# Attention and channel mixing on one core: parts of the beginning reordered, a later pace in the last unit, two projection blocks moved from unit 1 to unit 0

## What is computed

```
x = x + layernorm(attention(layernorm(x)))
    q, k, v = x @ w_q.T, x @ w_k.T, x @ w_v.T          # 16 heads of 16
    out = softmax(q k^T / 4) v;  out @ w_o.T
x = x + layernorm(ffn(layernorm(x)))
    xr, xk = mixes of x with the token before it (mu_r, mu_k)
    sigmoid(xr @ W_r.T) * (square(relu(xk @ W_k.T)) @ W_v.T)
```

## Time and profile before

| | before |
|---|---|
| median of 3 runs | 1273.29 us (1273.29 to 1273.8) |
| the profiled execution's own time | 1274.69 us |
| its span, first to last instruction | 1272.9 us |
| PE matmuls busy | 1252.4 us (98%) |
| ACT busy | 1067.7 us (84%) |
| DVE busy | 779.1 us (61%) |
| POOL busy | 276.4 us (22%) |
| mean granted TensorE clock | 0.998 |

### The profile page before, as it was taken

How to read it: one execution, slowest core, us unless ns; L and a number is a source line. 1 busy time by engine, 2 the same in 40 slices (tenths; PEclk the granted TensorE clock), 3 DMA queues, 4 the chain that set the end, 5 groups by cost and what they waited for, 6 DMA issues and landing times.

```text
span 1272.9 us, 25486 instructions
## 1 busy us (share of the span) xinstructions
PE 1252.4 (98%) x10604; PEld 603.3 (47%) x10604; DVE 779.1 (61%) x1725; ACT 1067.7 (84%) x1159; POOL 276.4 (22%) x356
## 2 busy tenths in 40 slices
PE   8999999999999999999999999999999999999997
PEld 5544454454544444454544544444444445534344
DVE  6543747758465773847567584666747466463737
ACT  4788888888888888888888888888888888898872
POOL 3000212222211321222121221223222122222211
PEclk9999999999999999999999999999999999999999
DMA  4455553317712194124733166321871129400001
GB/s 153 115 144 166 98 129 78 101 51 126 124 52 84 52 180 87 52 66 106 144 68 113 42 116 125 73 84 51 143 124 51 35 75 174 85 1 20 15 1 34
DMA packets 61797, 112.70 MB, mean 89 GB/s; under 512 B 6512, under 2 KB 31344, under 8 KB 61616
## 3 DMA queue, kind: packets, MB, share of 16 engines
q1 hardware_dynamic: 61360, 109.60, 38.8%
q10 hardware_dynamic: 288, 1.05, 0.3%
HBM read 68.42 MB, written 41.94 MB: 87 GB/s over the span
## 4 chain that ended last, share of the span: by engine, by line
PE 93%; DVE 3%; ACT 2%; DMA 1%; POOL 0%; issue 0%; ACTq 0%; DVEq 0%
PE O L602 38%; PE S L583 26%; PE M L353 14%; PE M L340 11%; PE M L250 3%; ACT PT L590 1%; DVE sth L701 1%; DMA A<-w_dram 1%; PE M L483 1%; DVE A L710 0%; PE S L1016 0%; POOL rsh L706 0%; DVE QS L474 0%; ACT QS L471 0%; DVE A L914 0%
## 5 line engine op out<-in xcount | busy, mean ns | idle before, releaser
L590 ACT ACTIVATE PT<-S 128x1024 f32<-128x1024 f32 x1024 | 1003.5, 1026 | 156.8 <-PE S L583 156.2
L602 PE MATMUL O<-PT,V 128*17 128x512 f32 x4096 | 538.9, 598 | 0.0
L583 PE MATMUL S<-QS,KS 50*128 50x512 f32 x2048 | 465.4, 450 | 3.2 <-ACT PT L590 3.2
L583 PEld LDWEIGHTS S<-QS,KS 50*128 50x128 f32 x2048 | 211.0, 183 | 452.7 <-ACT PT L590 375.2
L602 PEld LDWEIGHTS O<-PT,V 128*17 128x17 f32 x4096 | 67.8, 95 | 139.5 <-issue 137.7
L705 POOL TENSOR_SCALAR veh<-mvh 128x2 f32<-128x2 f32 x96 | 22.3, 232 | 491.3 <-DVE mvh L703 490.1
L914 DVE SCALAR_TENSOR_TENSOR A<-Z,M 128x512 f32<-128x512 f32 x30 | 20.4, 682 | 159.6 <-PE M L353 159.6
L340 PE MATMUL M<-xnT,WH 64*128 64x512 f32 (+1 forms) x504 | 110.7, 393 | 1.1 <-DVE WL L985 1.1
L353 PE MATMUL M<-WH,xnT 64*128 64x256 f32 (+1 forms) x496 | 83.0, 278 | 0.0
L353 PE MATMUL M<-WH,cT 64*128 64x256 f32 (+1 forms) x496 | 82.1, 278 | 0.5 <-DVE rec L661 0.4
L353 PE MATMUL M<-WH,C 64*128 64x256 f32 (+1 forms) x496 | 81.8, 278 | 0.0
(11 more groups left out here) (130 smaller groups left out, 1610.0 us busy)
## 6 DMA issues: line engine op xcount, KB each, us to landing
scr<-p SPq DMA_DIRECT2D x124, 256.0 KB
QS<-scr SPq DMA_DIRECT2D x56, 256.0 KB, 6.7
KS<-scr SPq DMA_DIRECT2D x56, 256.0 KB, 11.0
QS<-scr SPq DMA_DIRECT2D x70, 128.0 KB, 6.0
KS<-scr SPq DMA_DIRECT2D x68, 128.0 KB, 8.5
xA<-x_dram SPq DMA_DIRECT2D x16, 512.0 KB, 7.0
xB<-x_dram SPq DMA_DIRECT2D x16, 512.0 KB, 7.2
out_dram<-xB SPq DMA_DIRECT2D x15, 512.0 KB, 3.4
```

The lines of the kernel that those rows point to most:

```text
L583: fn = lambda e, p=p, a=a, rows=rows: e.matmul(PS[p][:, a, :], KS[qd][rows, p, kt * 128:kt * 128 + 128], QS[qd][rows, p, hf * 512:hf * 512 ...
L590: e_fn = lambda e, p=p: e.activation(PT[i % 2][:, 2 * p:2 * p + 2, :], PS[p][:, :, :], ACT.Exp, scale=SCALE)
L602: fn = lambda e, j=j: e.matmul(PO[32 * j:32 * j + 17, :], V[b % 2][:, kt, 4 * qd + j, :], PT[i % 2][:, j, :], start=(kt == 0), stop=(kt == 7))
```

## The change

There are three parts.

1. The beginning. The norm of the second 512 tokens goes from POOL to DVE, two tiles of it after the splitting of the widened weights, two after the sums for the range test. The splitting of wv goes ahead of D00, block V0 goes between T11 and E10, and the splitting of wq and wk goes between E10 and E01.
2. AHEAD: blocks Q10 and K10 of batch 1 are put at the end of unit 0's list, and taken out of unit 1's. Units 2 to 15 keep their lists.
3. In the last unit the age of 2 holds for the first 14 steps and not for the first 5.

```diff
-        def ln1_norm(b, g, eng=dve):
-            for t in range(4 * g, 4 * g + 4):
-                d = eng.op(lambda e, t=t: e.tensor_scalar(xA[:, t, :], xA[:, t, :], mv[:, t, 0:1],
+        def ln1_norm(b, g, tiles=range(4)):
+            for t in (4 * g + t for t in tiles):
+                d = dve.op(lambda e, t=t: e.tensor_scalar(xA[:, t, :], xA[:, t, :], mv[:, t, 0:1],
...
+        AHEAD = " Q10 K10"
...
         ln1_norm(0, 0)
-        ln1_norm(0, 1, pool)
         for i in range(2):
...
+        ln1_norm(0, 1, (0, 1))
         for word in ("T00", "T01"):
             alone(0, 0, word)
...
+        split_weights(["wv"])
+        ln1_norm(0, 1, (2, 3))
         alone(0, 0, "D00")
         alone(0, 0, "E00", sum_heads)
         alone(0, 0, "T10")
         alone(0, 0, "D10", sum_all)
         alone(0, 0, "T11")
-        split_weights(["wv"])
+        alone(0, 0, "V0")
         alone(0, 0, "E10")
+        split_weights(["wq", "wk"])
         flagged, = flagging
         alone(0, 0, "E01")
         alone(0, 0, "E11")
         load_xa(1)
         scores(0, 0, 1)
-        alone(0, 0, "V0")
-        split_weights(["wq", "wk"])
...
-                    for word in (EVEN, ODD)[hf].split():
+                    for word in (EVEN, ODD)[hf].split() if u > 1 else (EVEN + AHEAD, ODD.replace(AHEAD, ""))[hf].split():
                         block(b + 1, u - 1, word)
...
-                age = 2 if b + 1 == B and s < (5 if hf else 20) else 1
+                age = 2 if b + 1 == B and s < (14 if hf else 20) else 1
```

## The result

| | before | after |
|---|---|---|
| median | 1273.55 us (1273.29 to 1275.08, 4 runs) | **1283.62 us** (1279.69 to 1285.13, 4 runs) |
| the profiled execution's own time | 1274.69 us | 1279.69 us |
| its span | 1272.9 us | 1277.9 us |
| PE matmuls busy | 1252.4 us | 1254.5 us |
| ACT busy | 1067.7 us | 1068.8 us |

The ratio is 1.0072, 95% interval 1.0048 to 1.0096: slower, as forecast, but 1283.6 lies 2.7 above the end of the range. The profiled execution is the fastest of the four. Its time agrees with the forecast (1278.8) within 0.9; the other three had a mean granted clock of 0.995 or 0.996, against 0.999. So there are two things to explain: the 5 to 6 us of the profiled execution, and the 4 us that the usual one has on top.

What follows compares the result with a forecast made beforehand. The prediction took PE's queue, step by step, to bound the kernel. Its terms 0.2 + 1.95 + 2.15 + 1.0 + 0.2 = 5.5 us, put on the median 1273.29, gave 1278.8, range 1275.4 to 1280.9.

Steps and rivals of the forecast that it cites:

- The beginning, +0.2: Opening of the kernel: first exponential 1.35 later, 1.12 of waiting for weights regained, so Q00 starts 0.2 us later.
- Pieces of filler, +1.95: Steps 29 to 31 become filled, +1.25, and step 74 gets a second piece, +0.7: together +1.95 us.
- K10's bank, +2.15: Step 29: PE waits for the bank that Q01's cast frees late, behind Q00's store: +2.15 us, ends 0 and 2.3.
- y0, +1.0: Step 35: two more casts delay the last quad's turn, so PE waits for cT at y0: +1.0 us, ends 0 and 2.5.
- Step 74, +0.7: Step 74 gets a second piece of filler: +0.7 us, counted within the +1.95 for filler.
- The last unit, -1.7 + 1.9: Last unit and tail: last values 1.7 us earlier, then 1.9 more behind them; together +0.2, ends -1.0 and +0.8.
- PE's clock: Rival: granted clock halves behind new idle stretches of PE, +1.7 us, giving 1280.5; chance 0.2.
- both holes: New PE idle stretches: about 2.3 us before the second step's scores, and 2.15 us in step 29.
- The argument against it: Against the clock rival: the idle 1.12 us ahead of 33.67 cost no clock; no row shows where cost begins up to 2.
- the stores land in time: Rival, end of unit 0: Q00's store lands within 4.7 us, bank free, sum 2.35, giving 1275.6; chance 0.17.

Runs made afterwards that it cites:

- the change again: The whole change run once more with no edit: 1283.5 us (1280.53 to 1287.81, 5 runs), ratio 1.0084 to before.
- the kernel with both edits: All three parts of the change, with V1 ahead of the second step's first scores and unit 0's load of x at step 28, not 20: 1277.19 us.
- part 1 alone: The kernel before with only the edits of the beginning: 1276.59 us (1273.88 to 1278.45, 10 runs), ratio 1.0021.
- the fill of part 1's hole: The beginning's edits only, plus two matmuls of no use in PE's idle time behind the first scores: 1274.84 us, ratio 1.0003; five matmuls gave 1276.37.
- part 1 with V1 in the hole: The beginning's edits only, with block V1 taken ahead of the second step's first scores: 1272.96 us (11 runs), ratio 0.9994 to before.
- second profile: The kernel with only the beginning's edits, unchanged and profiled once more: 1275.92 us at a clock of 0.996.
- the change, once more: The whole change, unedited, profiled one more time: 1281.86 us at a clock of 0.996.

## Why the prediction was wrong, point by point

**The sum of the terms was near.** It was made for 1274.69, an execution with the early half-clock stretch, and gave 1280.2. After's profile, without that stretch, is 1279.69; against the executions of before near 1273.3 it is 6.4 more, where 5.5 was forecast. The table explains it: 0.5 + 5.7 - 1.7 + 1.9 = 6.4. The forecast put its sum on the median, 1273.29, for 1278.8.

- *The beginning, +0.2.* Right, +0.17 like for like, 0.5 with no early stretch on either side.
- *Pieces of filler, +1.95, and K10's bank, +2.15.* The mechanism was right, the bank's size was not: of the 2.6 of steps 29 to 31 the slots' 1.25 leave 1.35, of which 1.14 is seen as waiting. The forecast took over the store's time from before's profile, where it was issued 4.7 ahead of step 28's values. This distance is not fixed: it is 5.3 in after, 6.4 in the change again (PE waits 0.47) and 3.4 in the kernel with both edits (PE waits 2.30).
- *y0, +1.0.* Measured 1.40. *Step 74, +0.7.* Measured 1.02. The 0.66 of step 70, a wait for v's copy on DVE, was missed. These errors cancel the bank's: 5.1 forecast between the opening and unit 3, 5.7 measured.
- *The last unit, -1.7 + 1.9.* Right in both parts, -1.66 and +1.88.

**The step that failed is PE's clock: it stood at nothing in the sum, and as a rival it was priced and weighed too low.** The prediction named both holes, with lengths of 2.3 and 2.15 (measured 2.61, and 0.5 to 2.3), priced them together at one stretch, +1.7, and gave this 0.2. Even so the rival comes to 1280.5, 3.1 under the measured median. The runs show a stretch behind each hole: 1.5 for the first at the first values, which Q00 and V1 feel in full (part 1 keeps this to the end, the whole change gave 0.66 of it back in step 29 where the second stretch stayed away), and 0.6 net for the second. With both the change took 1281.86, 2.2 more than with none. And it is not the rarer case: in part 1 alone 8 executions of 10, and in after 3 of 4, have the lower clock; the fill of part 1's hole took it away. Behind step 29 the stretch is shown by one trace, and that hole wasn't filled to test it. The argument against it was that a hole of 1.12 cost nothing; but the new hole was twice that, and the only row with a longer idle stretch had the half clock behind it. That row should have carried the chance. A second fault: the fastest execution was forecast, and the median asked for.

By the Trainium skill, TensorE: Matmul & The Clock Gate (Part 1), the clock falls when PE is idle. The rows agree as to what comes behind what, and show that it falls behind such a hole in some executions of one program and not in others.

By the Trainium skill, DMA: Bandwidth & Descriptors (Anatomy of one DMA), a DMA that GpSimd issues takes about 2.0 us plus its bytes at 436 GB/s; an estimate of 2.6 for a store of 0.25 MB follows from it. These stores are issued by SP, and after's took 107.81 - 101.36 = 6.45 to its cast; so the rows disagree in this stretch, as the prediction had said, and the rival "the stores land in time" (1275.6) fell.

**Open.** The traces with lower clocks explain times up to 1281.9. The usual execution of the change takes 1283.6 at 0.995; the early stretch can be added to the other two (0.95 in before's opening, 0.54 in part 1's, 35.87 with it and 35.33 without), but there is no trace of such an execution, and the remaining 0.8 to 1.2 isn't settled. Executions of 1285 to 1287.8 are not explained either. Nor is it shown why a store takes 5.7 us and more to its cast when the load of x is away.

## What to carry to other kernels

Count an idle stretch of the bounding engine twice: its length, and the half-clock work that may follow it, when that work is on the path; a block that is moved out of such a place takes its cover with it. A hole that is closed with a block that was due anyway (V1) gains both. And a wait that ends at a time set by a DMA swallows what was gained ahead of it, so price a gain only up to the next such wait. Before one profile is taken for the usual execution, its clock is worth comparing with those of all the others: after's profile, at 0.999, was the exception.

The version that came out ahead is part 1 with V1 in the hole: 1272.96 against 1274.79 of before and 1283.5 of the change. Its interval against before still touches 1, so that it is better than before is probable, not shown.

## What was not expected of the hardware

The same program gets the half clock behind a hole in one execution and not in the next: after 2.61 idle, part 1 had it in its second profile and not in its first. In step 29 it came behind 1.58 idle (the change, once more) and stayed away behind 2.30 (all parts with both edits). So the length of a hole didn't tell alone. The early stretch stands behind a wait for the weights that ends near 7.7 us: PE was idle there for 1.9 to 2.1 in the four profiles that have it, and for 0.9 to 1.7 in the ten that don't. And before's own executions lie, but for a few, in two groups, 1273.2 to 1274.0 and 1274.7 to 1275.3, mostly at 0.998 or 0.999 and at 0.997 or 0.998, its profile with the early stretch among the second.
